# A macaron layer on one core: the last two chunks' end ordered by 128-row tiles and per engine, with chunk 6's first projection blocks put inside the last attention body

## What is computed

```python
x = x + 0.5 * ffn(layernorm(x))
x = x + attention(layernorm(x))
x = x + 0.5 * ffn(layernorm(x))
```

```python
logits = xf @ W_router.T;  probs = softmax(logits)
topk_p, topk_i = top_k(probs, 2);  topk_p /= sum(topk_p)
h = einsum('td,erd->ter', xf, lora_A)
lora_out = einsum('ter,eor,te->to', h, lora_B, w) * 2.0
return xf @ W_base.T + b_base + lora_out
```

## Time and profile before

| what | value |
|---|---|
| median of 3 runs | 1145.43 us (1144.08 to 1145.93) |
| the profiled execution's own time | 1146.65 us |
| its span, first to last instruction | 1144.9 us |
| mean granted TensorE clock | 0.961 |
| busy share of the span: PE, DVE, ACT, POOL | 92%, 73%, 63%, 26% |
| PE busy in 40 slices, the last two (of 28.6 us each) | 6 and 4 tenths |

### The profile page before, as it was taken

How to read it: one execution, slowest core, us unless ns; L and a number is a source line. 1 busy time by engine, 2 the same in 40 slices (tenths; PEclk the granted TensorE clock), 3 DMA queues, 4 the chain that set the end, 5 groups by cost and what they waited for, 6 DMA issues and landing times.

```text
span 1144.9 us, 16020 instructions
## 1 busy us (share of the span) xinstructions
PE 1057.5 (92%) x5776; PEld 465.2 (41%) x5776; DVE 836.3 (73%) x1107; ACT 726.5 (63%) x1361; POOL 294.6 (26%) x485
## 2 busy tenths in 40 slices
PE   5989887999999999999999999999999999998647
PEld 3768652344334332334333333343343334333335
DVE  4766679777777778887787688878877887781284
ACT  5556533667865787676767576766766676768411
POOL 5355647212510150230041004103200140041010
PEclk9988886999999999999999999999999999999869
DMA  7122341021111114112211121211113112100300
GB/s 257 38 91 90 91 114 39 24 60 49 43 54 31 49 34 137 39 42 66 66 33 31 50 89 31 66 53 49 31 31 97 42 41 73 54 11 33 120 0 37
DMA packets 70507, 68.31 MB, mean 60 GB/s; under 512 B 15132, under 2 KB 52508, under 8 KB 70428
## 3 DMA queue, kind: packets, MB, share of 16 engines
q1 hardware_dynamic: 70172, 67.15, 19.4%
q10 hardware_dynamic: 256, 0.13, 0.0%
HBM read 41.95 MB, written 24.63 MB: 58 GB/s over the span
## 4 chain that ended last, share of the span: by engine, by line
PE 76%; DVE 12%; ACT 5%; POOL 3%; issue 2%; DMA 1%; SPq 1%; ACTq 0%; DVEq 0%; POOLq 0%
PE ps_out L1541 20%; PE ps_score L1529 19%; PE ps_max L1510 17%; PE ps_fill L1466 5%; DVE neg_max L1337 4%; PE ps_fill L1495 3%; ACT probs L1035 2%; PE ps_fill L1448 1%; PE ps_fill L1470 1%; DVE neg_max L1134 1%; DVE zd L1208 1%; PE ps_fill L1434 1%; PE ps_out L1466 1%; PE ps_fill L1440 1%; DMA bias_half<-b 1%
## 5 line engine op out<-in xcount | busy, mean ns | idle before, releaser
L1035 ACT ACTIVATE probs<-ps_score 128x512 f32<-128x512 f32 x992 | 539.2, 597 | 258.3 <-PE ps_score L1529 256.5
L1337 DVE TENSOR_REDUCE neg_max<-ps_max 128x1 f32<-128x1024 f32 x480 | 570.8, 1218 | 165.0 <-PE ps_max L1510 163.0
L1529 PE MATMUL ps_score<-qst,kst 99*128 99x512 bf16 x992 | 308.1, 386 | 1.7 <-ACT probs L1035 1.3
L1510 PE MATMUL ps_max<-kst,qst 96*128 96x512 bf16 x1024 | 288.8, 388 | 16.0 <-DVE neg_max L1134 5.9
L1541 PE MATMUL ps_out<-probs,v_ring 128*32 128x512 f32 x2048 | 274.4, 608 | 6.8 <-ACT o_sb L1044 4.3
L1529 PEld LDWEIGHTS ps_score<-qst,kst 99*128 99x128 bf16 x992 | 76.0, 97 | 264.6 <-ACT probs L1035 221.9
L1510 PEld LDWEIGHTS ps_max<-kst,qst 96*128 96x128 bf16 x1024 | 90.9, 98 | 143.2 <-DVE neg_max L1337 18.6
L869 POOL CAST shift<-neg_max 128x16 bf16<-128x16 f32 x32 | 8.7, 273 | 389.4 <-DVE neg_max L1337 385.0
L1541 PEld LDWEIGHTS ps_out<-probs,v_ring 128*32 128x32 f32 x2048 | 40.9, 108 | 94.5 <-issue 86.1
L965 ACT ACTIVATE xn<-xc,ln_shift,rstd 128x512 f32<-128x512 f32 x48 | 38.5, 813 | 33.5 <-POOL ln_shift L765 22.3
L1466 PE MATMUL ps_fill<-wb_h,xt_h 128*128 128x512 f32 x84 | 46.5, 553 | 1.5 <-DVE xc L1324 0.8
(11 more groups left out here) (254 smaller groups left out, 1292.8 us busy)
## 6 DMA issues: line engine op xcount, KB each, us to landing
qst<-q_dram SPq DMA_DIRECT2D x192, 64.0 KB, 2.2
att_dram<-o_sb SPq DMA_DIRECT2D x31, 256.0 KB, 2.1
q_dram<-zm SPq DMA_DIRECT2D x24, 256.0 KB, 2.6
kst<-k_dram SPq DMA_DIRECT2D x192, 32.0 KB, 2.2
xc<-x SPq DMA_DIRECT2D x8, 512.0 KB, 4.0
x_dram<-xc SPq DMA_DIRECT2D x8, 512.0 KB, 2.9
xc<-x_dram SPq DMA_DIRECT2D x8, 512.0 KB, 4.6
out<-xc SPq DMA_DIRECT2D x8, 512.0 KB, 2.8
```

The lines of the kernel that those rows point to most:

```text
L1035: act.activation(probs[:, kt % 2, j, :], score_bank(i, uu, j), ACT.Exp, scale=1.0 / HD ** 0.5).then_inc(probs_ready, 1)
L1337: dve.tensor_reduce(neg_max[:, uu % 2, t:t + 1], ps_max[max_slot(uu, pos)][:, :, :], AXY, ALU.max, negate=True).then_inc(max_read, 1)
L1510: last = pe.matmul(ps_max[slot][:, half, :], qst[0:SR, r, j, q * P:(q + 1) * P], kst[0:SR, r, half * 512:half * 512 + 512], start=True, st ...
L1529: pe.matmul(score_bank(i, uu, j), kst[0:SR + PARTS, uu, kt * P:(kt + 1) * P], qst[0:SR + PARTS, uu, j, :], start=True, stop=True).then_inc ...
```

## The change

The order of the tail is written out by hand for each engine, in five tables of groups `chunk steps`. Letter A is chunk 6, which moves to the buffers with number 1 (free since the front), B is chunk 7 in the buffers with number 0. Two tables put parts of A and B into the last body; the key is the half slot:

```diff
-TAIL_LAG = 7
-TAIL_ON_DVE = ("clamp", "sum", "bias", "add")
+TAIL_ON_DVE = ("clamp", "sum", "add")
+TAIL_PE_ORDER = """
+B Oa0 Ob0 | A Oa1 | B Oa1 | A Ob1 | B Ob1 | A T1a T1b RT HT0 RU HT1 | B T1a | A FFa0 FFa1 FFa2 | B T1b | A WR
...
+LAST_FILL = {42: ["NR"], 45: ["NL"], 50: ["E0"], 52: ["EH"], 54: ["EL"], 57: ["Oa0"], 58: ["Ob0"]}
+OTHER_FILL = {50: ["NR"], 53: ["NL"], 60: ["E0"]}
```

```diff
+        if s < 2:
+            return 4 + 2 * (1 - self.slot) + s, 0
+        bnk = ((0, 3), (1, 2))[self.slot][s % 2]
+        return bnk, before + (0 if bnk else 2 * NF + LOOP_BACKS * NB) + (s - 2) // 2
...
+                    halves = ((0, 1, 2), (3,)) if ch.tail else ((0, 1), (2, 3))
+                    for c in halves[piece]:
...
+                if pos in ("E0", "N3"):
+                    c = slice(0, ch.whole) if pos == "E0" else slice(ch.whole, DC)
+                    if pos == "E0":
+                        dve.wait_ge(att_loaded[ch.att], ch.att_need)
+                        dve.wait_ge(recip_loaded[ch.att], ch.att_need)
+                    else:
+                        dve.wait_ge(tail_late_loaded[s], 2 * 16)
+                        dve.wait_ge(last_sums_loaded[s], 16 * REP)
+                        dve.reciprocal(recip_t[ch.att][:, c, :], recip_t[ch.att][:, c, :]).then_inc(last_recip_ready[ch.att], 1)
+                        dve.wait_ge(last_recip_ready[ch.att], 1)
+                        dve.wait_ge(last_out_loaded[s], 16 * REP)
+                    dve.tensor_tensor(att_t[ch.att][:, c, :], att_t[ch.att][:, c, :], recip_t[ch.att][:, c, :],
+                                      ALU.mult).then_inc(att_normed[s], 1)
```

SP loads A's blocks at slot 18 and B's at slot 22 (both at slot 27 before), the four heads of block 3 that are known at slot 26 (`load_late`, outputs and sums unreversed), and the last unit's heads as before. In the tail ACT issues A's four copies of sums (`SUMS`), makes B's `EH`, and then issues B's four:

```diff
+                    if last and slot == 18:
+                        sp.wait_ge(att_low_ready[0], 2 * LOOP_BACKS)
+                        load_att(TAIL[0])
+                        load_x1(TAIL[0], x1_loaded[1])
+                    if last and slot == 22:
                         sp.wait_ge(filler_ready[0], load_next.written("T1b"))
...
+TAIL_ACT_ORDER = """
+A SUMS | B EH SUMS | A H3 | B H3 | A C0 | B C0 | A C1 | B C1 | A LN1c LN1d T1a T1b RT | B LN1c | A HT1 R2 | B T1a LN1d T1b | A
...
+TAIL_DVE_ORDER = """
+B EL | A N3 | B N3 | A L3 | B L3 | A Oa1 | B Oa1 | A Ob1 C0 C1 G0 G1 P0 P1 AD0 AD1 LN1a | B Ob1 | A LN1b | B C0
```

More of the change, by code:

```diff
@@ L163, in __init__ @@
         self.mb0 = n * NF if self.front else NF * FRONT_PAIRS + n * NB
+        self.rows = NCH - 2 + (1 - slot) if tail else n
+        self.whole = 3 if tail else DC
+        self.att_need = 16 * (DC * self.att_use + self.whole)
     def on_dve(self, work):
@@ L207, in alone_order, with tail_order @@
         order += [(chunk, step) for step in steps]
+    return order
+def tail_order(text):
+    chunks = {"A": Chunk("back", 1, 0, tail=True), "B": Chunk("back", 0, LOOP_BACKS, tail=True)}
+    order = []
+    for group in text.split("|"):
+        name, *steps = group.split()
+        order += [(chunks[name], step) for step in steps]
     return order
@@ L529, in fill @@
                     load_recip(ch)
-                if not ch.front and pos == "FFb4":
-                    a = n if not ch.tail else NCH - 2 + s
+                if ch.tail and pos in ("FFa4", "FFb4"):
+                    t = "ab".index(pos[2])
+                    sp.wait_ge(filler_read[ch.bank(pos[:3])[0]], ch.bank(pos[:3])[1] + 1)
+                    sp.dma_start(out[bass.ds((ch.rows * CT + t) * P, P), :], xc[s][:, t, :]).then_inc(xc_stored[s], 16)
+                if not ch.front and pos == "FFb4" and not ch.tail:
+                    a = ch.rows
                     sp.wait_ge(filler_read[ch.bank("FFb")[0]], ch.bank("FFb")[1] + 1)
@@ L545, in load_att @@
                 s, n = ch.slot, ch.n
-                a = n if not ch.tail else NCH - 2 + s
+                a = ch.rows
                 for i in range(2):
-                    sp.wait_ge(att_stored[i], (a // 2) * 64 + 64 - (16 if ch.tail and i == 1 else 0))
+                    sp.wait_ge(att_stored[i], (a // 2) * 64 + 64 - (16 if ch.tail else 0))
                 heads = att_dram[bass.ds(a // 2, 1), :, :, (a % 2) * CH:(a % 2) * CH + CH].rearrange(
                     "o k (j x) t -> (o k j) x t", x=2 * HD)
-                known = H - REP if ch.tail else H
+                known = ch.whole * (P // HD)
                 groups = P // H
@@ L571, in load_recip @@
                 s, n = ch.slot, ch.n
-                a = n if not ch.tail else NCH - 2 + s
-                known = H - REP if ch.tail else H
+                a = ch.rows
+                known = ch.whole * (P // HD)
                 sp.wait_ge(recip_stored[ch.att], (ch.att_use + 1) * 16)
-                for c in range(DC):
-                    h0, h1 = c * (P // HD), min((c + 1) * (P // HD), known)
+                for c in range(ch.whole):
+                    h0, h1 = c * (P // HD), (c + 1) * (P // HD)
                     sp.dma_start(recip_t[ch.att][0:(h1 - h0) * HD, c, :],
@@ L656, in body @@
                     fill(item)
-            tail = [Chunk("back", 0, 6, tail=True), Chunk("back", 1, 0, tail=True)]
             for s in range(2):
@@ L832, in fill @@
                     expert_weights(ch)
-                if pos in ("LN2a", "LN2b") and ch.alone:
+                if (pos in ("LN2a", "LN2b") and ch.alone) or (pos in ("LN1a", "LN1b") and ch.tail):
                     norm_tile(ch, "ab".index(pos[3]))
@@ L836, in fill @@
                     norm(ch, 0 if pos == "LN1b" else 1)
-                if pos == "LN1d" and not ch.on_dve("bias"):
+                if pos == ("BI" if ch.tail else "LN1d") and not ch.on_dve("bias"):
                     add_bias(ch, 0)
@@ L960, in fill @@
                     t = "cd".index(pos[3])
[L961 to L962 removed]
+                    if ch.alone and (pos[2] == "2" or ch.tail):
+                        act.wait_ge(tile_rstd_ready[s], ch.norm_base(t) + 4)
                     else:
@@ L1240, in fill @@
                     else:
-                        dve.wait_ge(residual[s], n * 2 + 2)
+                        dve.wait_ge(residual[s], n * 2 + (1 if ch.tail else 2))
+                if pos == "LN1b" and ch.tail:
+                    dve.wait_ge(residual[s], n * 2 + 2)
                 if pos in ("LN2a", "LN2b"):
@@ L1358, in body @@
                             copy_rows(i, uu + 1, use, at)
-                    if last and slot == 8 * UB - 4:
-                        for ch in (Chunk("back", 0, 6, tail=True), Chunk("back", 1, 0, tail=True)):
-                            invert_sums(ch)
                     for pos, t in pairs[:1]:
@@ L1421, in fill @@
                 tok = slice(t * P, (t + 1) * P)
-                if ch.alone and ch.front and piece == 0:
+                if ch.alone and piece == 0:
                     inputs = {"RT": ("T1a", "T1b"), "RU": ("RT",), "VK": ("T2a", "T2b"), "Q0": ("T2a", "T2b")}
```

165 lines of the change are left out of this document (99 added, 66 removed).

## The result

Four runs of the changed kernel took 1133.85, 1134.21, 1132.51 and 1128.34 us, median **1133.18 us**; the kernel before, beside it on the same chip, 1145.11 us (1144.08 to 1145.93). The ratio is 0.9888 with a 95% interval of 0.9858 to 0.9918: faster, by 1.1%. The forecast was 1134.2 us with a range of 1130.5 to 1138.8.

The account below looks back on a forecast made before the run. Mostly full-speed PE bounds the kernel; its tail is first a DVE chain, then full PE. Tail -13.3, last store -0.7 and T0 +2.8 sum to -11.2 us: 1145.43 - 11.2 = 1134.2 us, range 1130.5 to 1138.8.

Parts of the forecast that it names:

- T0 + 2.8: Twelve added products in the last body delay T0, the end of ACT's copy of attention's last product, by 2.8 us.
- EH at nothing: ACT's added EH, 768 columns before slot 27's exponentials, costs 0 because PE has ffn work; 0.9 us without that cover.
- Chunk 6's low part at T0 + 10.4: In the tail, DVE finishes chunk 6's low part at T0 + 10.4, having waited about 3 us for chunk 7.
- third rival: Inverses return late through DRAM, so EH holds up attention; 3 us late would give 1137.2 us; chance 0.05.
- Two norms at 2.4: POOL's four small operations for each of chunk 6's two tiles take 2.4 us beside busy DVE, reaching T0 + 24.4.
- first rival: POOL and DVE hardly meet in the tail: norms 1.3 us a tile, bias meets nothing; 1131.0 us; chance 0.12.
- Low parts + 27.8: After the norms, ACT, transposes, their copy, low part and hand-overs bring chunk 6 to T0 + 27.8.
- The clock back at + 32: PE's full clock returns near T0 + 32 in the tail, 9.3 us after PE resumes work at about T0 + 23.
- 18.4 us of PE: From chunk 7's first transposes at T0 + 32.4, PE works 18.4 us without stopping, to T0 + 50.8.
- + 1.0 for the bias: POOL's bias meets DVE making chunk 6's expert weights, which PE awaits; 1.0 us taken between 0 and 1.3.
- second rival: POOL and DVE meet at each step of norms and bias: 3.5 us more, 1137.7 us; chance 0.18.
- fourth rival: The clock stays at 0.50 through the tail's ffn pieces, taking 36.8 us: 1152.6 us, slower than before; chance 0.03.

Follow-up runs that it names:

- e5: Changed kernel with chunk 6's low part put ahead of chunk 7's last product with the reciprocals on DVE: 1135.13 us, ratio 0.9898.
- e0: The changed kernel once more, with no edit: 1133.95 us, ratio 0.9892.
- e1: Changed kernel with chunk 6's twelve projection products moved from the body to the front of the tail: 1132.49 us, ratio 0.9885.
- e2: Changed kernel with the bias moved back from GpSimd to VectorE, behind w_rep: 1133.62 us, ratio 0.9908.
- e4: Changed kernel with thirty useless 512-column products on PE before chunk 6's transposes: 1132.35 us, ratio 0.9879.
- e7: Changed kernel with chunk 6's projection in the tail, useless products in PE's waits, reordered tail and both GpSimd biases after all four norms: 1134.34 us, ratio 0.9903.

## Why the prediction was right, step by step

The time came within 1.0 us, which is closer than its parts: some steps were off in opposite directions and cancelled, and that is luck.

- **T0 + 2.8.** It moved by 3.06. Of that 1.0 is the start of this run (first `o_sb` at 232.1 against 231.1), which no edit touches; the body grew by 2.1. The twelve products cost 2.7 by the bodies with and without them, so the step was right in size. The 0.6 us between 2.7 and 2.1 are less than the 1.6 by which the seven bodies with the products differ (845.8 to 847.4).
- **EH at nothing.** ScalarE did EH for 0.84 us from 1057.74 to 1058.58, directly behind the exponentials, without a wait. The inverses were there in time: E0 began at 1052.99, so 3.8 us were spare, not 2.3. The third rival is out.
- **Chunk 6's low part at T0 + 10.4, "about 3 us" the price of the order.** It came at + 9.4; ScalarE issued chunk 7's copies beside EH, which I had added up. The price was mis-read: e5 removed the wait and lost 0.8 us. DVE has work without a break from + 3.8 to + 10.0 and PE is in chunk 7's products until + 9.5, so nothing stood idle for it.
- **Statistics at + 19.5**: + 17.9, 1.0 of it from the step above.
- **Two norms at 2.4.** The first took 1.34 (1096.81 to 1098.15), the second 2.45 (1098.23 to 1100.68), and so in e0, e1, e2 and e5. DVE runs an evacuation from PSUM and then statistics beside the first, and clamps and a sum, with inputs in SBUF only, beside the second. The first and last operations of both norms (timeline of POOL):

```profile
1096.81 0.23 POOL L834 TENSOR_SCALAR var_eps<-meanvar 128x1 f32<-128x1 f32 x1 [42.06 <-DVE meanvar L1329]
...
1097.96 0.19 POOL L839 TENSOR_TENSOR ln_shift<-neg_mean,rstd 128x1 f32<-128x1 f32 x1
1098.23 0.56 POOL L834 TENSOR_SCALAR var_eps<-meanvar 128x1 f32<-128x1 f32 x1
...
1099.95 0.73 POOL L839 TENSOR_TENSOR ln_shift<-neg_mean,rstd 128x1 f32<-128x1 f32 x1
```

  "DVE is as busy here as there" was the mistake: DVE is busy beside both, so which operations meet counts, not how busy DVE is. The first rival had 1.3 for both, the second 3.0; neither.
- **Low parts + 27.8, chunk 7's transposes + 32.4**: + 25.3 and + 30.6. The 2.5 us gained above went on; I had left out a wait of 0.46 for the copy of the logits from the bank that HT0 writes.
- **The clock back at + 32.** This is the step whose form was wrong. There is no such moment: of eight profiles of the changed tail without dummies or with e4's alone, two have + 29.0 and + 29.5 and six + 35.5 to + 36.5, and the forecast lay between the two by chance. The Trainium skill, TensorE: Matmul & The Clock Gate, section "What's actually happening", says that the monitor of the engine's activity runs freely and "doesn't reset when your kernel starts"; two moments 6 us apart with one code agree with that, though the page gives half a microsecond for the shift and this case shows 6. The later return costs 2.0 us. Together with the start it may be why four runs of one kernel lie between 1128 and 1134; only one of the four was profiled.
- **18.4 us of PE, last product + 50.8, and + 1.0 for the bias.** From chunk 7's first transposes at 1109.41 to the last product's end at 1128.87 it was 19.5, 1.1 more than 18.4: 0.31 are PE's wait for `w_rep`, and in six of the twenty pieces the second product starts 0.31 to 0.34 behind the first in place of 0.23. The collision was 1.06 us long, as forecast, but only those 0.31 of it reached PE. So a sum that was 1.1 too small and a + 1.0 for which nothing more came cancelled, by luck: the last product came at + 50.1, the last evacuation at + 50.8 against 52.5, which is the 1.8 us that chunk 7's transposes came early.
- **The store - 0.7**: - 0.9.

The tail was forecast at -13.3 and measured at -15.0 with the early clock, -13.0 with the late one (e0).

The second rival was the rule of SBUF — State Buffer, section "Who interferes with whom", of the Trainium skill, at full strength. In the changed kernel it fits what is seen at chunk 6's second norm and at `w_rep`. e7 agrees with the page: three operations with two inputs in SBUF are lengthened by most of an addition of GpSimd (0.8 to 1.0 us of 1.25), the reciprocal isn't. `den`, with one input, is lengthened too; the same section says that a `tensor_scalar` can contend by its 2-port modes. I had priced the rule as an addition to each step and read it as holding for every operation of DVE, whereas it decides by pairs of operations. The fourth rival is out: the clock came back by + 36.5 in all eight profiles.
